# A kernel of two transformer blocks: in the first attention the tail of a batch's routing moves into the next batch's step 0 on VectorE, the scatters behind the normalisation of P, and two signals of their own are added

## The reference

```python
# layer 0, attention: 16 heads of 64; query i sees the keys j < i + 64
h = silu(x @ W1.T + b1) @ W2.T + b2
q, k, v = split(h @ Wg.T + bg)
attn = softmax(where(j >= i + 64, -inf, q @ k.T / 8))
x = layernorm(x + (attn @ v) @ Wo.T + bo)
# layer 1, 16 experts, the best 4 of each token
logits = -sum((x - keys) ** 2) + x @ rw.T + rb
topv, topi = top_k(logits, 4); w = softmax(topv)
x = layernorm(x + sum_k w[k] * expert[topi[k]](x))      # gelu MLP, 128 -> 512 -> 128
# layer 2: attention with 16 heads of 8 and LoRA; layer 3: a recurrence over the 16 batches
```

## Time and profile before

| | |
|---|---|
| median of 3 runs | 1431.74 us |
| lowest and highest run | 1426.88 and 1431.79 us |
| profiled execution, first to last instruction (span) | 1445.1 us |
| its mean granted TensorE clock | 0.960 of full speed |
| busy: PE (TensorE matmuls) | 1272.4 us, 88% |
| busy: DVE (VectorE) | 1014.5 us, 70% |
| busy: ACT (ScalarE) | 931.4 us, 64% |
| busy: POOL (GpSimd) | 770.7 us, 53% |

### The profile page before, as it was taken

One profiled execution on the slowest core, in us unless ns is written; L12 is line 12 of the kernel. 1 busy time (PEld: TensorE's weight loads), 2 busy tenths in 40 slices (PEclk: granted clock), 3 DMA queues, 4 the chain that ended last, 5 costly groups with the idle time before them and its releaser, 6 DMA issues.

```text
span 1445.1 us, 36685 instructions
## 1 busy us (share of the span) xinstructions
PE 1272.4 (88%) x9756; PEld 971.6 (67%) x9756; DVE 1014.5 (70%) x3763; ACT 931.4 (64%) x2825; POOL 770.7 (53%) x981
## 2 busy tenths in 40 slices
PE   7999999999999999984899998996787788788973
PEld 3777776777777777764899998993455455455652
DVE  2677777777777777775677776766787677678835
ACT  5878777777777778772465665653565555556644
POOL 1557777777777777775222121235466666664132
PEclk9999999999999999997899999997899989999997
DMA  9612222221112222221222223222323223222102
GB/s 340 206 60 74 73 73 73 73 73 54 47 51 72 69 71 71 73 74 58 62 71 82 77 82 90 81 79 65 80 58 78 67 53 85 58 61 64 36 1 59
DMA packets 149016, 110.98 MB, mean 77 GB/s; under 512 B 12833, under 2 KB 137249, under 8 KB 148770
## 3 DMA queue, kind: packets, MB, share of 16 engines
q1 hardware_dynamic: 139842, 92.45, 22.0%
q0 software_dynamic: 8192, 16.79, 4.1%
q10 hardware_dynamic: 864, 0.39, 0.1%
HBM read 47.27 MB, written 61.93 MB: 76 GB/s over the span
## 4 chain that ended last, share of the span: by engine, by line
PE 60%; DVE 10%; issue 8%; ACT 7%; another core or an unknown queue 4%; DMA 3%; SPq 3%; DVEq 3%; ACTq 1%; POOL 0%; POOLq 0%
PE psum L911 9%; PE psum L922 8%; PE psum L798 6%; PE psum L835 6%; PE psum L853 5%; PE psum L746 4%; PE psum L815 3%; PE psum L753 3%; PE psum L947 3%; PE psum L747 3%; ACT wall L1183 2%; PE psum L935 2%; PE psum L1018 2%; ACT P L1153 2%
## 5 line engine op out<-in xcount | busy, mean ns | idle before, releaser
L554 POOL TENSOR_SCALAR P<-P,rinv 128x192 f32<-128x192 f32 (+1 forms) x384 | 308.5, 816 | 158.7 <-DVE rinv L1335 151.7
L1153 ACT ACTIVATE P<-shifted,least 128x192 f32<-128x192 f32 (+1 forms) x512 | 240.2, 470 | 100.6 <-DVE least L1321 99.1
L1175 ACT ACTIVATE hid<-psum,wA 128x128 f32<-128x128 f32 x576 | 164.4, 368 | 123.8 <-PE psum L911 120.2
L1512 DVE TENSOR_REDUCE mx<-psum 128x2 f32<-128x512 f32 x256 | 165.2, 687 | 66.4 <-PE psum L1018 42.3
L1321 DVE CUSTOM_DVE_ANT_0 shifted<-psum,band 128x192 f32<-128x192 f32 (+1 forms) x512 | 168.9, 385 | 27.5 <-PE psum L798 27.2
L598 POOL DMA_INDIRECT yk<-xs,posc x128 | 125.6, 981 | 107.4 <-DVE wA L1473 57.6
L1183 ACT ACTIVATE wall<-psum 128x1024 f32<-128x1024 f32 x128 | 130.8, 1022 | 65.7 <-PE psum L935 47.5
L911 PE MATMUL psum<-xgT,wA 128*128 128x128 f32 x1152 | 156.0, 279 | 2.0 <-ACT hid L1175 1.4
L922 PE MATMUL psum<-wB,hid 128*128 128x128 f32 x1152 | 152.6, 276 | 0.0
L911 PEld LDWEIGHTS psum<-xgT,wA 128*128 128x128 f32 x1152 | 143.3, 195 | 3.2 <-ACT hid L1175 1.8
L835 PEld LDWEIGHTS psum<-ident,P 128*128 128x128 f32 x1024 | 117.6, 141 | 35.8 <-issue 29.4
(11 more groups left out here) (261 smaller groups left out, 2537.0 us busy)
## 6 DMA issues: line engine op xcount, KB each, us to landing
xs<-zrow SPq DMA_DIRECT2D x34, 1024.0 KB
xg<-xs SPq DMA_DIRECT2D x144, 64.0 KB, 1.8
xs<-yrow SPq DMA_DIRECT2D x144, 64.0 KB
wall<-in_wall SPq DMA_DIRECT2D x1, 8232.0 KB, 36.3
qkd<-parts SPq DMA_DIRECT2D x64, 96.0 KB
kst<-qkd SPq DMA_DIRECT2D x22, 128.0 KB
qst<-qkd SPq DMA_DIRECT2D x22, 128.0 KB
wall<-qkd SPq DMA_DIRECT2D x20, 128.0 KB
```

The costliest lines, as they stand in the source:

```text
L554: g.tensor_scalar(x, x, rinv[:, par, n:n + 1], None, ALU.mult).then_inc(s["pn_ready"], 1)
L1153: last = sc.activation(P[:, par, it, h, 0:w], shifted[:, par, it, h, 0:w], ACT.Exp, scale=-1.0, bias=least[:, par, n:n + 1], accum_out=row ...
L1175: sc.activation(hid[:, n % 4, f, :], up(n, f), ACT.Gelu, bias=wA[:, n % 4, F + f:F + f + 1]).then_inc(s["hid_ready"], 1)
L1512: v.tensor_reduce(out=mx[:, :, h], in_=SB[(par + 1 + h) % 3].rearrange("q (i n) -> q i n", i=TT), axis=mybir.AxisListType.X, op=ALU.max).t ...
```

## The change

The tail of the routing becomes a function `positions(b)` and is called on VectorE for batch b - 1 at the end of step 0 of body(b), behind `values`; only for the last batch does it stay in step 7. On GpSimd the scatters stand behind the normalisation of the same step and are dealt 1, 2, 2 and 3 to the steps 0 to 3, rather than 2 each ahead of it. Two signals are added: `lg_ready` behind the logits (L1329), for which TensorE's value projection of step 6 waits in place of `top_ready`, and `rank_ready` on the update of count (L1347), for which the value projection of step 0 waits in place of `pos_ready`, and so does the product with the LoRA factors behind the loop (L887). No arithmetic is changed.

```diff
--- before.py
+++ after.py
@@ -300,7 +300,7 @@
         names = """w_in xT_in0 xT_in1 xT_in2 xT_in3 wg_in rest_in x_in wall_in cst cst2 went_on hA_mm hA_act hB_mm h_ready
             qk_mm q_ev k_ev v_mm v_ev hv_ready
             scores shifted_ready exps rinv_ready pn_ready pn1_ready pt_mm ptA_ev ptB_ev pv_mm ot_ev wo_mm res_ready bo_mm
-            var_ready pow_ready x1c_ready m_x x1T_ready m_l mask_ready m_r pos_ready xsq_ready x1_kept scat exp_w top_ready
+            var_ready pow_ready x1c_ready m_x x1T_ready m_l lg_ready mask_ready m_r rank_ready pos_ready xsq_ready x1_kept scat exp_w top_ready
             ksq_ready rmat_ready b2_kept a_done plan_ready zrow_ready plan_out plan_in filled
             b2_mm xg_in0 xg_in1 xg_in2 xg_in3 tin_mm xgT_ready wA_ready wB_ready up_mm hid_ready dn_mm yrow_ready ys_out0 ys_out1
             cw_in lora_mm c_set cleared mrow_in to_full to_free st_full exps1 s_full max_done pv_full o_free full0 full1 free0 free1 a1_ready parts_ready
@@ -536,14 +536,6 @@
                     if p == 5 and is_batch(b, -1):
                         need(pool, "x1c_ready", b)
                         g.tensor_copy(x_all[:, bass.ds((b - 1) * TT, TT), :], rows_of(b - 1)[:, :, :]).then_inc(s["x1_kept"], 1)
-                    if p < 4 and is_batch(b, -2):
-                        if p == 0:
-                            need_alone(pool, "pos_ready", b - 1)
-                            need_alone(pool, "filled", 32 * (b - 1))
-                        for k in (2 * p, 2 * p + 1):
-                            nc.gpsimd.indirect_dma_start(
-                                out=xs, out_offset=bass.IndirectOffsetOnAxis(pos[:, k:k + 1], 0),
-                                in_=rows_of(b - 2)[:, k // TOPK, :], in_offset=None).then_inc(s["scat"], 16)
                     if is_pair(b, p, 0):
                         par = p % 2
                         for h in range(2):
@@ -552,6 +544,14 @@
                                 n = 2 * h + it
                                 x = P[:, par, it, h, 0:(N - WINDOW if it == 0 else N)]
                                 g.tensor_scalar(x, x, rinv[:, par, n:n + 1], None, ALU.mult).then_inc(s["pn_ready"], 1)
+                    if p < 4 and is_batch(b, -2):
+                        if p == 0:
+                            need_alone(pool, "pos_ready", b - 1)
+                            need_alone(pool, "filled", 32 * (b - 1))
+                        for k in ((0,), (1, 2), (3, 4), (5, 6, 7))[p]:
+                            nc.gpsimd.indirect_dma_start(
+                                out=xs, out_offset=bass.IndirectOffsetOnAxis(pos[:, k:k + 1], 0),
+                                in_=rows_of(b - 2)[:, k // TOPK, :], in_offset=None).then_inc(s["scat"], 16)
 
             batch_loop(pool, 2, B - 1, 3, body)
             pool.wait_ge(s["scat"], 16 * B * TT * TOPK)
@@ -816,7 +816,7 @@
                             last.then_inc(s["wo_mm"], 1)
 
                     if p == 0 and has(b, 0) and has(b, -1):
-                        need(pe, "pos_ready", b - 1)
+                        need(pe, "rank_ready", b - 1)
                         vproj(4 * b + 1, 0, 1)
                     if p == 2 and is_batch(b, 0):
                         vproj(4 * b + 2, 1, 0)
@@ -855,7 +855,7 @@
                             last.then_inc(s["pv_mm"], 1)
                     if p == 6 and is_batch(b, 1):
                         need(pe, "hv_ready", b + 2)
-                        need(pe, "top_ready", b)
+                        need(pe, "lg_ready", b)
                         vproj(4 * b + 4, 0, 0)
 
             def after_attention(b, p):
@@ -884,7 +884,7 @@
                 b2 = wall[:, e, WA + FC * D:WA + FC * D + 1].to_broadcast([128, D])
                 mm(psum[:, e * D:(e + 1) * D], b2, ident[:, :], start=True, stop=True).then_inc(s["b2_mm"], 1)
             pe.wait_ge(s["cw_in"], 128)
-            pe.wait_ge(s["pos_ready"], B)
+            pe.wait_ge(s["rank_ready"], B)
             for k in range(4):
                 last = mm(MIS[1][:, k * D:(k + 1) * D], lora_a[:, k, :], lora_b[:, k, :], start=True, stop=True)
             last.then_inc(s["lora_mm"], 1)
@@ -1300,6 +1300,24 @@
                 cs = slice(512 * half, 512 * half + 512)
                 v.tensor_tensor(V[:, jt, cs], M[:, :], bv[:, cs], ALU.add).then_inc(s["v_ev"], 1)
 
+            def positions(b):
+
+                v.drain()
+                need(dve, "exp_w", b)
+                v.reciprocal(wsum[:, :], wsum[:, :])
+                for it in range(TT):
+                    v.tensor_tensor(junk[:, it * TOPK:(it + 1) * TOPK, :], hot[:, it, :, :],
+                                    rank[:, it:it + 1, :].to_broadcast([128, TOPK, E]), ALU.mult)
+                v.drain()
+                v.tensor_reduce(out=posf[:, :], in_=junk[:, :, :], axis=mybir.AxisListType.X, op=ALU.add)
+                v.drain()
+                if isinstance(b, int) and b == B:
+                    need(dve, "scat", 16 * TT * TOPK * (b - 1))
+                v.tensor_copy(pos[:, :], posf[:, :]).then_inc(s["pos_ready"], 1)
+                v.tensor_copy(pos_all[:, bass.ds((b - 1) * TT * TOPK, TT * TOPK)], posf[:, :])
+                for it in range(TT):
+                    v.tensor_scalar(gate_all[:, bass.ds(b - 1, 1), it * TOPK:(it + 1) * TOPK].rearrange("q o k -> q (o k)"), wexp[:, it, :], wsum[:, it:it + 1], None, ALU.mult)
+
             def body(b):
                 for p in range(8):
                     par, par1 = p % 2, (p - 1) % 2
@@ -1326,7 +1344,8 @@
                         need(dve, "xsq_ready", 2 * b)
                         need(dve, "exp_w", b - 1)
                         for it in range(TT):
-                            v.scalar_tensor_tensor(lg[:, it, :], M[:, it * E:(it + 1) * E], xsq[:, it:it + 1], rconst[:, :], ALU.subtract, ALU.add)
+                            last = v.scalar_tensor_tensor(lg[:, it, :], M[:, it * E:(it + 1) * E], xsq[:, it:it + 1], rconst[:, :], ALU.subtract, ALU.add)
+                        last.then_inc(s["lg_ready"], 1)
                         v.drain()
                         for it in range(TT):
                             v.max(top[:, it, :], lg[:, it, :])
@@ -1344,7 +1363,7 @@
                         need(dve, "m_r", b)
                         v.tensor_tensor(rank[:, :, :], M[:, 0:2 * E].rearrange("q (i e) -> q i e", i=TT), count[:, :].rearrange("q (o e) -> q o e", o=1).to_broadcast([128, TT, E]), ALU.add)
                         v.drain()
-                        v.tensor_tensor(count[:, :], count[:, :], M[:, 2 * E:3 * E], ALU.add)
+                        v.tensor_tensor(count[:, :], count[:, :], M[:, 2 * E:3 * E], ALU.add).then_inc(s["rank_ready"], 1)
                         v.tensor_tensor(rank[:, :, :], rank[:, :, :], first_row[:, :].rearrange("q (o e) -> q o e", o=1).to_broadcast([128, TT, E]), ALU.add)
                     if p == 3 and is_batch(b, -1):
                         need(dve, "wo_mm", 8 * b)
@@ -1367,6 +1386,8 @@
                         values(4 * b + (2 + p // 2), 1, p // 2 - 1)
                     if p == 6 and is_batch(b, 1):
                         values(4 * b + 5, 0, 0)
+                    if p == 0 and is_batch(b, -2):
+                        positions(b - 1)
                     if not is_batch(b, -1):
                         continue
                     if p == 3:
@@ -1381,22 +1402,8 @@
                         for it in range(TT):
                             last = v.tensor_scalar(rows_of(b - 1)[:, it, :], res[:, it, :], mv[:, it, 0:1], rstd[:, it:it + 1], ALU.subtract, ALU.mult)
                         last.then_inc(s["x1c_ready"], 1)
-                    if p == 7:
-                        v.drain()
-                        need(dve, "exp_w", b)
-                        v.reciprocal(wsum[:, :], wsum[:, :])
-                        for it in range(TT):
-                            v.tensor_tensor(junk[:, it * TOPK:(it + 1) * TOPK, :], hot[:, it, :, :],
-                                            rank[:, it:it + 1, :].to_broadcast([128, TOPK, E]), ALU.mult)
-                        v.drain()
-                        v.tensor_reduce(out=posf[:, :], in_=junk[:, :, :], axis=mybir.AxisListType.X, op=ALU.add)
-                        v.drain()
-                        if isinstance(b, int) and b == B:
-                            need(dve, "scat", 16 * TT * TOPK * (b - 1))
-                        v.tensor_copy(pos[:, :], posf[:, :]).then_inc(s["pos_ready"], 1)
-                        v.tensor_copy(pos_all[:, bass.ds((b - 1) * TT * TOPK, TT * TOPK)], posf[:, :])
-                        for it in range(TT):
-                            v.tensor_scalar(gate_all[:, bass.ds(b - 1, 1), it * TOPK:(it + 1) * TOPK].rearrange("q o k -> q (o k)"), wexp[:, it, :], wsum[:, it:it + 1], None, ALU.mult)
+                    if p == 7 and isinstance(b, int) and b == B:
+                        positions(b)
 
             batch_loop(dve, 2, B - 1, 2, body)
```

(1 more changed line is left out.)

## The result

The changed kernel takes 1469.5 us (median of 4 runs, 1469.0 to 1471.6) against 1429.3 us before (4 runs on the same chip, 1424.6 to 1431.8): a ratio of **1.0304, 95% interval 1.0278 to 1.0329**, slower by 40 us. (The ratios in this document are recorded with the runs and aren't the quotients of two medians; here that would be 1.028. The two differ by up to 0.3%.) Forecast were 1450 us and a range of 1437 to 1467. The direction and the place of the loss were right, its size was half of what came, and the measured time lies above the range.

The account below looks back on a forecast made before the run. TensorE was taken to set the pace in the first attention. Gains of 13.7, 2.8 and 1.0 us against losses of 6.5 (step 1) and 29.4 (step 5 stall) gave +18.4 us: 1450 us, range 1437 to 1467.

Parts of the forecast that it names:

- Step 0: TensorE's step 0 falls from 5.68 to 4.64 us without the tail ahead of PT; 13.7 us gained altogether.
- The tail in step 1: The moved tail delays the PT copy, so TensorE's transposes L835 wait 0.5 us in 13 batches; 6.5 us lost.
- lg_ready: The earlier signal frees value projection L753 in step 6 from waiting; 0.2 us in 14 batches, 2.8 us gained.
- The power: GpSimd's L535 comes only behind the scatters, so VectorE waits 1.8 us at L105.
- The stall is 1.8 to 2.65; I take 2.1: Step 5 waits per batch for the late power and for the scatters' landing before x1c; 29.4 us lost.
- Low for 3.4 us, it costs 1.7 us each time; in none to about half of 14 batches, typically five: Size of the clock's fall from 2.4 to 1.2 GHz after TensorE's stop in step 5; 9 us added.
- the case without a fall of the clock: The main forecast: 1450 us, nothing counted for a lower clock; chance 0.50.
- rival A: The clock falls too, after TensorE stands some 2 us in step 5: 1459 us, at most 1466; chance 0.28.
- The phase's end: End of the first attention, behind the batches: 1 us gained, between 4 gained and 2 lost.
- The sum: Terms -13.7 - 2.8 - 1.0 + 6.5 + 29.4 = +18.4 us on 1431.7, giving 1450 us.

Follow-up runs that it names:

- lg_only: Kernel before with the lg_ready signal alone, the tail left in step 7: 1427.4 us, ratio 0.9999.
- order_only: Kernel before with only the scatters moved behind the normalisation and dealt 1, 2, 2, 3, tail left in step 7: 1470.6 us, ratio 1.034.
- own_source_1223: own_source with the scatters dealt 1, 2, 2, 3 as in the changed kernel: 1491.8 us, ratio 1.045.
- power_first: Changed kernel with the power L535 in step 3, between the normalisation and the three scatters: 1466.0 us, ratio 1.026.
- filler: Changed kernel with two extra 512-column matmuls on TensorE where it waits for x1c in step 5: 1454.9 us, ratio 1.019.
- split_tail_2: own_source with the tail cut in three between VectorE's reciprocals, steps 0 to 2; scatters dealt 1, 2, 1, 2, 1, 1 from step 1: 1409.0 us.
- own_source: Changed kernel with scatters reading their own copy of x1c, dealt 1, 2, 2, 1, 1, 1 to steps 0 to 5: 1421.0 us, ratio 0.9952.
- tail_only: Changed kernel with the scatters ahead of the normalisation again, two a step: 1498.8 us, ratio 1.050.

## Why the prediction was right about the place and wrong about the size

**Step 0, right.** 4.64 to 4.65 us against 4.64 forecast. Each step 0 inside the loop is 1.03 us shorter.

**The tail in step 1, right, slightly small.** I took 0.5 us; 0.54 to 0.62 came (5.10 to 5.17 against 4.56). The PT copy starts 1.67 us into step 1 (235.18 against 233.51), forecast 1.69.

**lg_ready, right in the changed kernel, for a reason that stays argued.** 0.36 us less in step 6, 0.12 more in step 7: 0.24 against 0.2 taken. lg_only shows that it is worth nothing while the tail is in VectorE's chain.

**The power, right.** L105 late by 1.87 us against 1.8. order_only shows that GpSimd's order makes 1.2 us of it without the moved tail, own_source_1223 that the landing has no part in it.

**"The stall is 1.8 to 2.65; I take 2.1", mis-sized.** It measured 2.44: 1.87 of waiting for the power, and 0.57 because x1c started 1.62 us behind L105 and not 1.05. The 0.34 above my 2.1 did not come from the landing, as the text had it: the landing takes 1.29 us from the instruction's end (power_first), so x1c could have been written 1.1 us earlier. It came from two small instructions behind the power. L105 took 0.54 us and L109 0.53, against 0.15 and 0.35 in the kernel before and 0.15 and 0.16 in power_first. L535 is followed at once by a normalisation on GpSimd (254.30), with which they run side by side; but in the kernel before L105 ran beside one too, and took 0.15 us.

**"Low for 3.4 us, it costs 1.7 us each time; in none to about half of 14 batches, typically five": this is the step that failed**, and with it the choice of the case without a fall of the clock as the likeliest: the sum of 1450 us has nothing for it. The clock fell in 8 of 13 batches. Three cost 1.7 us, but five cost 3.1 to 3.3, because the clock stayed low for 6.8 us. Against 41.08 us, the mean of the four batches without a fall behind batch 2, the eight add 1.70 + 3.13 + 3.24 + 3.28 + 3.29 + 1.64 + 1.69 + 3.13 = 21.1 us. The prediction's rival A had 9 us for this and an upper end of 16, though seven falls at its 1.7 us make only 12. Filler shows by intervention that the stop of TensorE is the cause: with the stop cut to 0.58 us none of the 13 batches has it.

**The phase's end, wrong.** I took 1 us gained, between 4 gained and 2 lost. From step 7 of batch 15 to the experts nothing changed, and batch 15 itself lost 4.2 us (for which the sum had about 1.5, a stall of 2.1 less 0.62 in step 0): TensorE stands for 4.16 us in its step 5, and the clock falls during that stop.

**The sum.** Without the falls the 13 batches cost 44.3 - 21.1 = 23 us, 1.8 each, forecast 13 x 1.36 = 18; the clock 21, forecast 0; batch 15 another 4. That is 48 of the 48.6 us by which the experts start later; 40 came at the median. The 8 between lie behind this stage or in executions that have no trace, and stay open. The bounds were also drawn too narrow: taken outright, stall, step 1, L753 and the end give 1434 to 1468 us and not 1439 to 1464. The two profiled spans differ by 23.1 us only (1445.1 and 1468.2): the profiled execution of the kernel before lay 16 us above its median, and its second attention, which the change doesn't touch, took 466.1 us there (979.0 to 1445.1) against 444.1 in the profile after (1024.1 to 1468.2). The granted clock had fallen in several stretches there in both, more often in the profile before. The stage tables, not the spans, carry the comparison.

**Open.** Why the clock stays low for 3.4 us at one time and for 6.8 at another is not settled by these runs, nor what decides in which batches it falls. In the changed kernel it fell in batches 6 to 11, 13 and 14 and held in 2 to 5 and 12, behind stops of 2.37 to 2.40 us in all of them, so something besides the length of the stop decides. The small instructions' 0.54 us go together with the late power in three kernels (changed, order_only, own_source_1223), in each of batches 2 to 15, and are absent in power_first; no run isolated their cause.

## What to carry to other kernels

When work is moved out of one engine's critical chain, count the whole queue of every engine that it feeds, up to the next instruction somebody else waits for: here four normalisations, eight scatters and the power were counted to within 0.1 us, and the power that was needed last stood at the end. A stop of TensorE of about 2 us a pass is to be priced twice, once for the stop and once for the half clock behind it, and the second can be the larger. A tail of small VectorE work was free here once it was cut to the length of waits that existed anyway (split_tail_2). A copy of a buffer that DMAs read and every pass rewrites brought nothing by itself (own_source_1223); it paid when it allowed the scatters to be dealt further on (own_source).

## What the runs showed of the hardware that I had not expected

- At this length of stop the clock fell in some batches and not in others, with no order that these runs explain: with stops of 1.85 us (power_first) it fell in 9 of 13 batches, with 1.9 (order_only) in 3, with 2.4 in 8 (changed) and in 11 (own_source_1223), with 4.1 (tail_only) in all, with 0.58 (filler) in none, each in one profiled execution. In the changed kernel TensorE began at full clock after the stop and lost it while busy, within 0.6 us in six of the eight batches and 2.0 to 2.1 us after the start in the other two (6 and 13).
- Back at work without a pause, TensorE was kept at 1.2 GHz for 3.4 or 6.8 us. The Trainium skill (TensorE: Matmul & The Clock Gate, HAM oscillation) describes pauses that make every pass start cold. The traces agree that a pause in a pass costs the clock, but here the pass begins at full clock and not every pass is hit; the pauses, 1.85 to 2.4 us, are shorter than the one in its example.
- A scatter of 64 KB issued by GpSimd was known to have landed 1.29 us after its instruction's end, 2.25 us after its start. The Trainium skill (DMA: Bandwidth & Descriptors, Anatomy of one DMA) has about 2 us of fixed cost, which agrees if it is counted from the start; I had counted it from the end.
- Two instructions of VectorE on 128 x 2 elements (L105, L109) took 0.53 to 0.56 us behind a late power, with a normalisation just begun on GpSimd, while L107 between them kept its 0.16. Without the late power L105 took 0.15, also beside a normalisation (kernel before), and L109 0.35 (kernel before) or 0.16 (power_first).
